# One 96-row matmul in place of three 32-row matmuls in the low-rank correction of a dense layer

## What is computed

```python
logits = jnp.einsum('bsd,ed->bse', x, gate_W) + gate_b
top1 = jnp.argmax(jax.nn.softmax(logits, axis=-1), axis=-1)
base = jnp.einsum('bsd,fd->bsf', x, wi_W) + wi_b
for i in range(lora_A.shape[0]):                                    # 8 experts, rank 4
    lora = jnp.einsum('bsr,fr->bsf', jnp.einsum('bsd,rd->bsr', x, lora_A[i]), lora_B[i])
    inter = jax.nn.relu(base + lora)
    expert_out = jnp.einsum('bsf,df->bsd', inter, wo_W) + wo_b
    out = out + (top1 == i)[..., None] * expert_out
```

## Time and profile before

| what | us |
|---|---|
| median of 3 runs | 1986.92 |
| lowest and highest of them | 1980.81, 1989.0 |
| the profiled execution: its span, the only time that its page gives | 2007.2 |
| busy in that span: PE, VectorE (DVE), ScalarE (ACT) | 1773.6, 1262.0, 975.4 |

### The profile page before, as it was taken

How to read it: one execution, slowest core, us unless ns; L and a number is a source line. 1 busy time by engine, 2 the same in 40 slices (tenths; PEclk the granted TensorE clock), 3 DMA queues, 4 the chain that set the end, 5 groups by cost and what they waited for, 6 DMA issues and landing times. The chain is left out here.

```text
span 2007.2 us, 32563 instructions
## 1 busy us (share of the span) xinstructions
PE 1773.6 (88%) x11808; PEld 1447.6 (72%) x11808; DVE 1262.0 (63%) x2310; ACT 975.4 (49%) x1739; POOL 528.7 (26%) x492
## 2 busy tenths in 40 slices
PE   6998899967799996699999969998899789798895
PEld 4667799922577775699999558886577566688884
DVE  6886488546245553588887566765434688656643
ACT  4652476413687671377776234443433255317730
POOL 2220343254333341222220630002000144213333
PEclk9998799988799996699999979999699899899997
DMA  3003377420100000567775220000000100026742
GB/s 109 17 17 126 121 255 248 132 61 0 49 1 12 6 12 25 203 225 229 246 238 169 81 102 1 1 1 1 22 1 1 57 12 12 30 79 208 235 127 81
DMA packets 97139, 178.32 MB, mean 89 GB/s; under 512 B 25184, under 2 KB 61946, under 8 KB 95914
## 3 DMA queue, kind: packets, MB, share of 16 engines
q1 hardware_dynamic: 85496, 146.00, 22.0%
q0 software_dynamic: 11232, 30.69, 5.2%
q10 hardware_dynamic: 288, 0.00, 0.0%
HBM read 149.38 MB, written 27.26 MB: 88 GB/s over the span
## 5 line engine op out<-in xcount | busy, mean ns | idle before, releaser
L1667 POOL DMA_INDIRECT f_block_rows_home<-normed_x,f_token_of_sb x138 | 168.3, 1220 | 451.4 <-PE psum L1713 324.5
L1693 PE MATMUL psum<-f_block_h_sb,f_w1h_home 128*128 128x256 f32 x736 | 211.4, 287 | 30.2 <-issue 10.7
L1693 PE MATMUL psum<-f_block_l_sb,f_w1h_home 128*128 128x256 f32 x736 | 206.8, 281 | 0.0
L1693 PE MATMUL psum<-f_block_h_sb,f_w1l_home 128*128 128x256 f32 x736 | 206.7, 281 | 0.0
L2316 PE MATMUL psum<-a_xT_home,context_w 128*128 128x256 f32 x704 | 182.2, 405 | 13.6 <-PEq L122 9.7
L1703 PE MATMUL psum<-f_w2h_home,f_hidden_h_home 128*128 128x256 f32 x644 | 187.4, 291 | 2.0 <-DVE f_hidden_l_home L1887 1.0
L1703 PE MATMUL psum<-f_w2h_home,f_hidden_l_home 128*128 128x256 f32 x644 | 181.7, 282 | 0.0
L1703 PE MATMUL psum<-f_w2l_home,f_hidden_h_home 128*128 128x256 f32 x644 | 181.7, 282 | 0.0
L1693 PEld LDWEIGHTS psum<-f_block_h_sb,f_w1h_home 128*128 128x128 f32 x736 | 140.8, 191 | 38.5 <-issue 28.6
L2316 PEld LDWEIGHTS psum<-a_xT_home,context_w 128*128 128x128 f32 x704 | 132.6, 198 | 45.3 <-issue 20.0
L2481 ACT ACTIVATE a_probsT_sb<-psum 77x1024 f32<-77x1024 f32 (+1 forms) x128 | 130.7, 1021 | 69.0 <-PE psum L2368 66.5
(11 more groups left out here) (314 smaller groups left out, 3986.6 us busy)
## 6 DMA issues: line engine op xcount, KB each, us to landing
f_w_sb<-in_f_w SPq DMA_DIRECT2D x161, 512.0 KB
sorted_y<-f_result_sb SPq DMA_DIRECT2D x69, 256.0 KB
normed_x<-f_xn_all SPq DMA_DIRECT2D x24, 256.0 KB, 2.1
f_b_row_sb<-in_f_b SPq DMA_DIRECT2D x46, 128.0 KB
f_w_sb<-in_f_w SPq DMA_DIRECT2D x23, 256.0 KB
f_block_rows_home<-normed_x,f_token_of_sb POOLq DMA_INDIRECT x138
residual<-in_x SPq DMA_DIRECT2D x8, 256.0 KB, 6.2
context_w<-in_a_wk SPq DMA_DIRECT2D x2, 1024.0 KB, 5.0
```

Of the source, the lines that this page charges most:

```text
L1667: nc.gpsimd.indirect_dma_start(block_rows[b % 2][:, h, :], None, xs, bass.IndirectOffsetOnAxis(ap=column, axis=0)).then_inc(sems[f"rows_in ...
L1693: last = nc.tensor.matmul(hid_ps(q)[:, m, :], w, rhs, start=(j == 0), stop=(j == len(parts) - 1))
```

## The change

The 32 low-rank columns of lora_A stand three times in `wr`, so that `route` makes u three times (104 columns in place of 40), and lora_B is loaded three times, to partitions 0, 32 and 64. `um`, its turn and `u3` then have 96 rows. ScalarE rounds all 96 rows; VectorE overwrites rows 64 to 95 of `u3` with the low part of u, and rows 32 to 63 of `lb3` with the low part of lora_B. One matmul of 96 rows then adds the three products. In PSUM, `route`'s two halves stand 128 columns apart in place of 64.

```diff
-    NR = E * (1 + cfg["lora"])
+    LR = E * cfg["lora"]
+    NR = E + 3 * LR
...
-    loads = [(wr[:], dram[f"{name}_wr"]), (rb[:], dram[f"{name}_rb"].partition_broadcast(P))]
+    loads = [(wr[:, :, 0:E + LR], dram[f"{name}_wr"]), (rb[:], dram[f"{name}_rb"].partition_broadcast(P))]
+    if LR:
+        loads += [(wr[:, :, E + q * LR:E + (q + 1) * LR], dram[f"{name}_wr"][:, :, E:E + LR]) for q in (1, 2)]
...
-                last = nc.tensor.matmul(bank[:, h * 64:h * 64 + NR], xT[:, c, where], wr[:, c, :], start=(c == 0),
+                last = nc.tensor.matmul(bank[:, h * P:h * P + NR], xT[:, c, where], wr[:, c, :], start=(c == 0),
                                         stop=(c == DC - 1))
...
-        made = bank[:, 0:TPB * 64].rearrange("p (t r) -> p t r", r=64)
+        made = bank[:, 0:TPB * P].rearrange("p (t r) -> p t r", r=P)
...
-        t["uh"] = sb("uh", [32, TOKENS], F32R)
-        t["ul"] = sb("ul", [32, TOKENS], F32R)
+        t["u3"] = sb("u3", [96, TOKENS], F32R)
...
-    um = t["um"] = sb("um", [P, TILES, 32])
+    um = t["um"] = sb("um", [P, TILES, 96])
...
-        nc.vector.tensor_tensor(um[:].rearrange("p t (e r) -> p t e r", r=cfg["lora"]),
-                                t["front"]["low_rank"][:].rearrange("p t (e r) -> p t e r", r=cfg["lora"]),
-                                choose.oh1[:].unsqueeze(3).to_broadcast(with_r), ALU.mult).then_inc(sems["masked"], 1)
+        LR = E * cfg["lora"]
+        for q in range(3):
+            third = lambda v: v[:, :, q * LR:(q + 1) * LR].rearrange("p t (e r) -> p t e r", r=cfg["lora"])
+            last = nc.vector.tensor_tensor(third(um), third(t["front"]["low_rank"]),
+                                           choose.oh1[:].unsqueeze(3).to_broadcast(with_r), ALU.mult)
+        last.then_inc(sems["masked"], 1)
...
-    lb = sb("lb", [32, U, UNIT])
-    lbh, lbl = sb("lbh", [32, U, UNIT], F32R), sb("lbl", [32, U, UNIT], F32R)
-    ust = sb("ust", [32, 2, 512])
+    lb, lb3 = sb("lb", [96, U, UNIT]), sb("lb3", [96, U, UNIT], F32R)
+    ust = sb("ust", [96, 2, 512])
+    MIDDLE, LOWER = slice(32, 64), slice(64, 96)
...
-    u_ps = lambda k: psum[0:32, 4 + k % 2, :]
+    u_ps = lambda k: psum[0:96, 4 + k % 2, :]
...
-        sp.dma_start(lb[:], dram[f"{name}_lb"]).then_inc(sems["lora_in"], 16)
+        for q in range(3):
+            sp.dma_start(lb[32 * q:32 * q + 32, :, :], dram[f"{name}_lb"]).then_inc(sems["lora_in"], 16)
...
-                terms += [(w[:, u, cols], v[:, tok]) for w, v in ((lbh, uh), (lbh, ul), (lbl, uh))]
+                terms.append((lb3[:, u, cols], u3[:, tok]))
...
-            high(uh[:, chunk(k)], u_ps(k), "u_high")
+            high(u3[:, chunk(k)], u_ps(k), "u_high")
...
-        act.wait_ge(sems["lora_in"], 16)
-        high(lbh[:], lb[:], "lora_high")
+        act.wait_ge(sems["lora_in"], 48)
+        high(lb3[:], lb[:], "lora_high")
...
-            low(ul[:, chunk(k)], ust[:, k % 2, :], uh[:, chunk(k)], "u_low")
+            low(u3[LOWER, chunk(k)], ust[LOWER, k % 2, :], u3[LOWER, chunk(k)], "u_low")
...
-        low(lbl[:], lb[:], lbh[:], "lora_low")
+        low(lb3[MIDDLE], lb[MIDDLE], lb3[MIDDLE], "lora_low")
```

More of the change, by code:

```diff
@@ L1250, in experts @@
     HC = UNIT // P
-    xT, xh, xl, uh, ul = front["xT"], t["xh"], t["xl"], t["uh"], t["ul"]
+    xT, xh, xl, u3 = front["xT"], t["xh"], t["xl"], t["u3"]
     gate = env["tg"][:, 4 + n:5 + n]
```

## The result

The changed kernel's median is 1953.33 us (1948.69 to 1958.55), that of the kernel before in the same session 1986.23 us: a ratio of 0.9849, interval 0.9824 to 0.9875. That is 30 us less (25 to 35), where 25.2 us had been forecast. Two later sessions gave 0.9859 (0.9827 to 0.9890) and 0.9876 (0.9859 to 0.9892), 28 and 25 us.

What follows compares the result with a forecast made beforehand. TensorE was taken to bound f2's main loop, VectorE the stretch before it. Loop saving 27.5 us, less 1.5 (start) and 0.8 (`route`), gave 25.2 us: 1986.9 to 1961.7 us, range 1954 to 1969, with the two cheaper rivals 1952 to 1975.

Steps and rivals of the forecast that it cites:

- The loop: f2's main loop: a bank's group falls from 2.47 to 1.61 us, saving 27.5 us in 32 groups.
- The 2 us either way: First groups of f2's loop at 1.2 GHz: allowance for when the clock rises, left out of the 27.5 us.
- The reading of the group: Nine matmuls of a bank: 0.23 us each, plus 0.40 us as two breaks of 0.20 where row counts change.
- 96 rows like 77: Weight loads in f2's loop: 96 rows beside 128 make no breaks, as at a 77-row load; 0.86 us saved a group.
- the first rival: f2's loop: 96 rows beside 128 still lose 0.40 us a group; saving 12.4 us, 1974.5 us; chance 0.10.
- The start: f2's start, ahead of the loop: two more products and a larger turn cost 1.5 us, lora_B's further loads nothing.
- The products: f2's start: VectorE multiplies `um` three times, two more products at 0.61 us each, 1.2 us on the path.
- The turn: Turn directly ahead of f2's loop: loading 96 columns of weights takes 0.3 us more.
- `route`: Rows at the end of a2: 104 columns cost nothing, copy 0.14 us more, tail 0.1; 0.8 us in all.
- The second rival: f2's start and `route`: columns exposed (7 us), lora_B loads late (2.3 us); saving 15.9 us, 1971.0 us; chance 0.08.
- ScalarE: Emptying banks in f2's loop: keeps up, its wait for PE per bank falling from 1.20 to some 0.3 us.
- the rival on the slower side: Clock falls in or behind f2's loop; whole loop at 1.2 GHz gives 2059 us; chance 0.04.

Runs made afterwards that it cites:

- the reordered kernel: Kernel before with the same nine matmuls, the three 32-row ones first in banks 1 and 3, 32 row-count changes instead of 64: 1975.66 us, ratio 0.9962.
- the 64-row kernel: Changed kernel with its 96-row matmul cut to the first 64 rows, leaving out the product of u's low part: 1972.06 us, ratio 0.9940.

## Why the prediction was right

**The loop** was the large term, 27.5 us. Measured against a trace with less difference in the time at the low clock it is 26.5 to 27, against the trace on which the prediction stood 29.3, the excess being the late rise of the clock there. The 2 us either way that the prediction allowed for the clock were the right size.

**The reading of the group** was right in both parts. That 0.40 us in a bank was no matmul but two breaks, and that they came from the change of rows, was worked out from three idle marks and one load without a mark; the reordered kernel (4.53 us a pair) and the 64-row kernel (0.20 us a change) show it. By the loops, 14.7 us of the gain are fewer matmuls (125.6 to 110.9) and 12.0 breaks (110.9 to 98.9); the 64-row kernel puts the breaks at 12.8.

**96 rows like 77** was the choice on which half of the gain hung. It was an argument from the nearest row, and that row was one of two kinds. The same trace has marks at 77 rows where the product has 32 columns, which the prediction leaves out:

```profile
75.06 0.59 PEld L2384 LDWEIGHTS psum<-a_probsT_sb,a_values_home 77*32 77x32 f32 x16 [0.16 <-issue]
76.06 0.20 PEld L2388 LDWEIGHTS psum<-identity,a_inv_of_sb 128*128 128x128 f32 x2 [0.41 <-issue]
```

The new matmul has 128 columns, like the 77-row load that the prediction chose. The choice held: the first rival, breaks that stay, would have shown groups of 2.01 us, and the 64-row kernel shows what that would have looked like: 1972.06 us where the rival had forecast 1974.5. The Trainium skill's rule (TensorEngine Tiling (Array Packing), Key Properties), that a change of mode drains the engine, agrees with the 0.20 us at 32 and 64 rows beside 128. A drain as such no trace shows, only the lost time; read strictly, with 96 rows as a mode of their own, the rule would have kept the breaks, and there were none.

**The start** was forecast at 1.5 us and took 1.7 to 1.8. The products were right to 0.01 us. The turn was dearer by 0.11 us and not 0.3. The rest, some 0.4 us, was missing from the sum: VectorE's instructions lie less close together, see below.

**`route`** had been priced at 0.14 us a sequence for the copy plus 0.1 at the end, 0.8 us in all. The copy was right (0.35 against 0.21), and the loads do set the pace at 104 columns while the clock is low. The turn behind `route` begins 0.10 us later in each sequence and not only at the last, so the period grew by 0.20 us there. But the term as a whole had the wrong sign. The prediction counted with the low clock to the end of the rows, and with 104 columns the clock rises before it: the rows take 0.1 to 0.6 us less and not 0.8 more. The second rival, exposed columns and late loads (9.3 us), is refuted by the 1.78 us and by ScalarE's second wait.

**ScalarE** was forecast to wait some 0.3 us a bank; it waits 0.35. After its rise, some 3.4 us into the loop, the clock stayed at 1.00 to the loop's end, so the rival on the slower side did not arise.

**The sum.** From the first turn of the rows to the loop's last product the changed kernel's three traces are 25.1 to 25.9 us shorter than that of the kernel before profiled again. The forecast was 25.2. That it is so near is partly luck: the loop gained somewhat less than 27.5 and the start cost more than 1.5, and `route`, which was to cost 0.8, made up for both.

**The times and the clock.** The ratios say 25, 28 and 30 us. The time of a run goes with the mean granted clock that is on record with it. At 0.934 the kernel before took 1986.7 us in the mean of 8 runs and the changed one 1959.4 in 3; at 0.940, 1976.5 in 4 and 1948.9 in 3. So 0.006 of clock go with some 10 us in either kernel, and at like clock the two are 27 to 28 us apart (at 0.935, 0.937 and 0.938, with one or two runs on one side, 25 to 30). Some 1.5 us of that the comparison makes itself (an estimate): the loop loses 27 us at full clock, which lowers the mean clock by 0.001 for the same time at the low level. What is left, some 26 us, is what the traces show between the rows and the loop's end, and no gain elsewhere is needed. Why one execution is granted a higher clock than another stays open.

## What to carry to other kernels

Before pricing a matmul by its duration, take the distance of the starts in a stream, and look at which weight loads have an idle mark with no wait behind it: where row counts change, the change itself can cost as much as a matmul. Stacking small products into one of more rows pays twice then, for the matmuls that go and for the breaks that go with them (here at 96 rows, not at 64), and the order of the terms alone gives half of the second part at no cost. Compare the stage that was changed, in more than one execution: the rest of this kernel moves by more than 10 us from one to the next. Where only times are at hand, compare runs of like granted clock.

## What was not expected

**Breaks go with 64 rows, too, and not with 96.** With one small matmul in a bank the two marks are 0.35 and 0.24 us, and the group still loses 0.40.

**VectorE's instructions stop overlapping around the rows 32 to 63 and 64 to 95.** In the earlier trace rows and between w1 low and x low 0 of the changed kernel, an instruction starts some 0.1 us before the end of the one ahead of it. In the changed kernel x low 0 starts at 1405.65 and lasts 1.22 us, and lora low, on rows 32 to 63, starts at 1406.90, after its end. The same gap follows lora low, u low 0, x low 1 and u low 1. The first four lie on the path to the turn of part 3, some 0.11 us each, which is what the start's sum was short of. The instructions on those rows also write over one of their inputs, which those of before did not, so whether the place of the rows or the overwriting is the cause was not told apart.
